# Weight splits of the last five experts moved to the second half of row 1, the clearing of the sorted rows moved to row 2, and twelve matmuls on cleared rows ahead of TensorE's first turn

## What is computed

```python
x = x + attn(layernorm(x))      # logits = Q K^T / sqrt(8); attn = sin(30 * logits) V; then Wo, bo
def expert(x, Wg, Wu, Wd): return silu(x @ Wg.T) * (x @ Wu.T) @ Wd.T     # 128 -> 256 -> 128
probs = sigmoid(x @ Wr.T + rb); scores, idx = top_k(probs, 2)
x = x + expert_shared(x) + sum over e of cw[..., e] * expert_e(x)         # x after a second layernorm
```

## Time and profile before

| | us |
|---|---|
| median of 3 runs | 456.49 |
| the profiled execution | 458.69 |
| span of the profiled execution, first to last instruction | 456.9 |
| PE busy in the span | 419.2 |
| ACT busy | 337.6 |
| DVE busy | 294.0 |
| POOL busy | 236.7 |

### The profile page before, as it was taken

How to read it: one execution, slowest core, us unless ns; L and a number is a source line. 1 busy time by engine, 2 the same in 40 slices (tenths; PEclk the granted TensorE clock), 3 DMA queues, 4 the chain that set the end, 5 groups by cost and what they waited for, 6 DMA issues and landing times.

```text
span 456.9 us, 12398 instructions
## 1 busy us (share of the span) xinstructions
PE 419.2 (92%) x4432; PEld 220.9 (48%) x4432; DVE 294.0 (64%) x999; ACT 337.6 (74%) x470; POOL 236.7 (52%) x308
## 2 busy tenths in 40 slices
PE   2899989999999999999999999999999988999972
PEld 1322222433433345554454455554544588998862
DVE  6778487456546254758676457786475567667894
ACT  1567968988989978788868887778788656765440
POOL 5261352120177333224867585426685778678851
PEclk9999989999999999999999999999999999999995
DMA  6027868917506642684246724992112256651221
GB/s 173 6 82 201 181 183 241 296 33 227 107 24 177 170 94 66 174 199 82 80 133 199 133 72 145 188 196 70 48 49 63 59 104 153 148 147 42 70 60 34
DMA packets 82187, 56.07 MB, mean 123 GB/s; under 512 B 28752, under 2 KB 76496, under 8 KB 82128
## 3 DMA queue, kind: packets, MB, share of 16 engines
q1 hardware_dynamic: 77824, 47.74, 41.6%
q0 software_dynamic: 3584, 7.35, 6.0%
q10 hardware_dynamic: 720, 0.20, 0.2%
HBM read 22.62 MB, written 27.13 MB: 109 GB/s over the span
## 4 chain that ended last, share of the span: by engine, by line
PE 63%; DVE 14%; issue 8%; ACT 7%; DMA 2%; POOL 2%; SPq 1%; DVEq 0%; ACTq 0%; POOLq 0%
PE o_ps L754 19%; PE score L741 10%; ACT attn L1018 4%; PE tile_ps L881 4%; PE tile_ps L883 4%; PE tile_ps L882 4%; PE tile_ps L906 3%; DVE hid L1351 2%; DVE x_all L1397 2%; PE r_ps L767 2%; DMA y_back<-in_wd 2%; PE r_ps L697 2%; PE r_ps L704 2%; PE tile_ps L908 2%; PE tile_ps L907 2%
## 5 line engine op out<-in xcount | busy, mean ns | idle before, releaser
L1018 ACT ACTIVATE attn<-score 128x1024 f32<-128x1024 f32 x237 | 231.7, 1031 | 22.5 <-PE score L741 22.1
L1576 POOL TENSOR_TENSOR hid_lo<-hid,hid_hi 128x256 f16<-128x256 f32 (+1 forms) x94 | 71.7, 763 | 128.0 <-DVE hid_hi L1359 116.4
L754 PE MATMUL o_ps<-attn,vals 128*32 128x512 f32 x1024 | 136.8, 606 | 0.5 <-ACT o_t L1025 0.5
L741 PE MATMUL score<-queries,keys 64*128 64x512 f16 x474 | 76.8, 384 | 4.6 <-ACT attn L1018 3.6
L1351 DVE SCALAR_TENSOR_TENSOR hid<-tile_ps,gate 128x256 f32<-128x256 f32 (+1 forms) x88 | 40.4, 459 | 49.3 <-ACT gate L1039 47.7
L1039 ACT ACTIVATE gate<-tile_ps 128x256 f32<-128x256 f32 (+1 forms) x88 | 36.3, 412 | 35.1 <-PE tile_ps L883 33.7
L881 PE MATMUL tile_ps<-xt,w_hi 128*128 128x128 f16 x244 | 43.7, 219 | 0.7 <-ACT y_sb L1051 0.7
L754 PEld LDWEIGHTS o_ps<-attn,vals 128*32 128x32 f32 x1024 | 20.2, 108 | 49.1 <-issue 48.0
L883 PE MATMUL tile_ps<-xt,w_lo 128*128 128x128 f16 x244 | 43.7, 219 | 0.0
L882 PE MATMUL tile_ps<-xt,w_hi 128*128 128x128 f16 x244 | 43.7, 219 | 0.0
L1044 ACT ACTIVATE hid_hi<-hid 128x512 f16<-128x512 f32 (+1 forms) x38 | 23.1, 607 | 27.8 <-DVE hid L1351 27.8
(11 more groups left out here) (226 smaller groups left out, 997.5 us busy)
## 6 DMA issues: line engine op xcount, KB each, us to landing
q_four<-q_parts SPq DMA_DIRECT2D x14, 256.0 KB
queries<-q_four SPq DMA_DIRECT2D x14, 256.0 KB
k_four<-k_minus SPq DMA_DIRECT2D x14, 256.0 KB
keys<-k_four SPq DMA_DIRECT2D x14, 256.0 KB
y_sorted<-y_sb SPq DMA_DIRECT2D x52, 64.0 KB
x_sorted<-zeros SPq DMA_DIRECT2D x2, 1472.0 KB, 8.5
queries<-q_three SPq DMA_DIRECT2D x14, 192.0 KB
keys<-k_three SPq DMA_DIRECT2D x14, 192.0 KB
```

Source lines behind the costliest of these rows:

```text
L741: mm = pe.matmul(sets[which][:, i, :], keys[b % 2][rows, 2 * j + h, kt * P:(kt + 1) * P], queries[b % 2][rows, 2 * j + h, :], start=True, ...
L754: mm = pe.matmul(o_ps[32 * i:32 * i + 32, :], vals[b % 2][:, kt, h:h + 32], attn[k % RING][:, i, :], start=(k == 0), stop=(k == UNITS - 1))
L1018: act.activation(attn[k % RING][:, 2 * (u % 2):2 * (u % 2) + 2, :], sets[SCORE_SET[b * SLOTS + u][0]][:, :, :], ACT.Sin, scale=SIN_SCALE). ...
L1576: pool.tensor_tensor(cells(hid_lo, d), cells(hid, d), cells(hid_hi, d), ALU.subtract).then_inc(lo_by_pool, 1)
```

## The change

The nine preparation slots, evenly spaced before (12, 16, ... 44), become a list: 12, 16, 20, 24 as before for experts 0 to 3, and 46, 49, 54, 56, 62 for experts 4 to 8. With them move the splits (two slots later) and the loads of experts 6, 7 and 8 (now at slots 49, 52 and 57, before at 31, 35 and 39). The two clears move from slots 48 and 50 to 66 and 68. PE gets a wait on a new semaphore, set when POOL has cleared `vals[0]`, and then 12 f32 matmuls of 128x128 on that cleared buffer into r_ps, whose result the first transposes overwrite.

```diff
-PREP_FIRST, PREP_EVERY = 12, 4
+PREP_AT = (12, 16, 20, 24, 46, 49, 54, 56, 62)
+PREP_FIRST = PREP_AT[0]
...
+WARM = 12
...
 def prep_at(a):
-    e, off = divmod(a - PREP_FIRST, PREP_EVERY)
-    return e if 0 <= e < EXP and off == 0 else None
+    return PREP_AT.index(a) if a in PREP_AT else None
...
+        vals_clear = sem("vals_clear")
...
-                if a in (SLOTS + 16, SLOTS + 18):
-                    clear((a - SLOTS - 16) // 2)
+                if a in (2 * SLOTS + 2, 2 * SLOTS + 4):
+                    clear((a - 2 * SLOTS - 2) // 2)
...
+            pe.wait_ge(vals_clear, 1)
+            for _ in range(WARM):
+                pe.matmul(r_ps[:, 0:P], vals[0][:, 0, 0:P], vals[0][:, 0, 0:P], start=True, stop=True)
             pe.wait_ge(ld_id, 16)
             xt1(0)
...
-            pool.memset(vals[0][:, :, :], 0.0)
+            pool.memset(vals[0][:, :, :], 0.0).then_inc(vals_clear, 1)
```

## The result

The changed kernel takes 455.09 us in the median of 20 runs (454.02 to 457.48), the kernel before 456.33 in 20 runs (455.33 to 458.16). The ratio is 0.9967, with a 95% interval of 0.9954 to 0.9980: faster by a third of a percent, about 1.5 us, where 6.1 us were forecast. The time lies above the range of 449.0 to 454.0. In a second comparison, with 12 executions of the changed kernel, the ratio was 0.9985 (0.9963 to 1.0007), which does not exclude no change. Ratios are taken from the executions that did not run in the slow state.

The account below looks back on a forecast made before the run. PE was taken to bound the kernel, busy 419.2 of 456.9 us. Start 2.4, seam 3.72, middle of row 1 0.38, late splits -0.4 summed to 6.1 us, taking the median from 456.49 to 450.4; range 449.0 to 454.0.

Parts of the forecast that it names:

- The seam: Between rows 0 and 1: PE's pause goes (2.13 us) and the clock does not fall (1.59), together 3.72 us.
- the late splits: Splits of experts 6 to 8, second half of row 1: PE may wait before its second `down`; 0.4 us lost.
- the median, 2.2 us below it, becomes 456.49 - 6.1: Final step: the whole 6.1 us, summed from the profiled execution, is taken off the median, giving 450.4 us.
- rival B: Row 1 to row 3's copy: late weights of experts 7 and 8 hold DVE again; 454.6 us, chance 0.14.
- Expert 8 at nothing: Before row 3's copy: expert 8's weights are rounded before DVE comes, so its split costs nothing.
- The burst: Start: twelve matmuls raise PE's clock early and it stays; first scores 2.4 us earlier, bounds 0 and 2.7.
- Rival A: Start: the clock is not there when the projections come; 451.4 us, or 452.8 with nothing won; chance 0.25.
- The middle of row 1: Without the split between pack_hi and pack_lo, `xt2` follows its scores; 0.38 us won, bounds 0 and 0.70.
- The clears: Issued behind expert 8's load and x's, they run from about 90 us in a stretch without q and k loads; worth 0.
- C: Row 1's key transfer or a later row waits for something fixed and the gain is given back; 456.5 us, chance 0.05.
- D: Slow loads of experts 7 and 8 hold DVE's list and PE behind it; slower, 458.9 at 10 us landing; chance 0.06.

Follow-up runs that it names:

- experiment 3: The kernel before, unchanged, run and profiled once more; ratio 0.9984 (0.9942 to 1.0025).
- again: The changed kernel, unchanged, run and profiled a second time; ratio to before 0.9985 (0.9963 to 1.0007).
- experiment 4: Changed kernel with experts 7 and 8 rounded and split in row 2 (slots 78, 81); ratios to before 0.9905, 0.9922, 0.9893 in three comparisons.
- experiments 2: The kernel before plus only the twelve matmuls at the start and their semaphore; ratio to before 0.9967 (0.9932 to 1.0002).
- Experiment 7: Changed kernel with experts 7 and 8 rounded and split in row 2, without the twelve matmuls; ratio to before 0.9955 (0.9936 to 0.9973).
- experiment 8: The changed kernel without the twelve matmuls, keeping its own preparation list and moved clears; ratio to before 0.9987 (0.9965 to 1.0009).
- experiments 1: The kernel before with only the list of preparation slots changed, clears and start as before; ratio to before 1.0140 (1.0074 to 1.0205).

## Why the prediction was wrong, point by point

- **The seam: right in mechanism, and in size for the execution it was read from.** Against the first profile of before the second stretch fell by 34.95 - 31.25 = 3.70 us; 3.72 were forecast. Against the second profile it is 2.06. The idle time is in all three profiles that had the pause (2.06, 1.93 and 1.73 us); the 1.59 of half clock in two of them (before and burst alone yes, before again no), and by the clocks in experiment 3 probably in fewer executions than that.
- **Two steps failed: the term of 0.4 us for the late splits, which cost 2.8 and is the largest error (next point), and "the median, 2.2 us below it, becomes 456.49 - 6.1".** In the second I took terms out of one execution and subtracted them whole from the median. The distance of 2.2 us was a warning: its size is that of the half clock (1.64) and the late rise (0.78) that I counted as gain. The typical run had lost less, so there was less to win. An estimate agrees: from the third marker to the end it is 352.5 us in the first profile of before, so the median of 456.33 has its third marker near 103.8, where the second profile has it (103.75, the first 106.18). For the seam the prediction gave 2.13 as the lower bound, for a clock that falls anyway; the case that came, by these signs, is a clock that in the typical execution of before does not fall at all. The sum should have said which terms hang on the clock and given them a chance.
- **The term mis-sized: the late splits, 0.4 us taken.** They cost 1.7 (changed), 3.2 (again) and 2.6 us (list and clears), the third stretch less 36.33: 2.5 in the mean. The middle's gain of 0.3 is already off these, so the late weights themselves cost 2.8; the medians of experiment 4 say 2.9. The mechanism of rival B and its landing were right: 89.4 on the clock of before was forecast, the first profile has 82.12 with 6.1 us won before it, 88.2. What was wrong is the middle value between 0 and 0.9, which had no row behind it, and the 1.30 us for a split: beside POOL's work it took 1.76 and, for expert 8 before row 3's copy, 2.37. The Trainium skill (SBUF — State Buffer, who interferes with whom) spoke for the longer one, and the trace agrees in direction: 1.76 is 1.30 plus 0.46, most of the one hidden_lo of 0.67 beside it, and 2.37 is 1.30 plus 1.07, most of the add of 1.27.
- **Expert 8 at nothing** was wrong for that reason: not its load (84.91, in time) but its split stood in the way, for 0.87 us.
- **The burst: 2.4 forecast.** 34.90 - 32.47 = 2.43 between the two profiles, and the first scores 2.49 earlier; but between the second profiles 0.54. Rival A's 0.25 fits what came: the rise was lost in 2 of 7 profiled executions with twelve matmuls. What was wrong is that 2.4 went into the sum whole, as if every execution kept it, and against one late rise: without a burst the clock rose anywhere from 13.0 to 16.2. The mean first kf is 34.27 in five profiles without and 32.79 in seven with it: 1.5 us, which is the 0.33% of experiments 2 and 7; experiment 8 gives less. The Trainium skill (TensorE: Matmul & The Clock Gate, part 1) says that the switch point differs from run to run; these rows agree, and I should have priced the term by it.
- **The middle of row 1: right.** 36.33 - 36.04 = 0.29 against 0.38.
- **The clears, forecast at 0: wrong in kind.** Moving them without the list was not run. They are a condition of the list, worth about 7 us with it (experiments 1 and 8).
- **Rivals C and D.** Nothing was absorbed later: from the third marker to the end it is 352.5 us in the first profile of before and 352.4 to 352.9 in the five of other kernels on chips where before takes 456 us. D did not happen in the changed kernel, but in its list alone.

Summed again by means: burst 1.5, seam 2.1, middle 0.3, late weights -2.8: 1.1 us, and on top what the clock's fall at the seam took from before. By two profiles in three that is 1.1, and the sum 2.2 would lie above both measurements, 1.5 (0.9 to 2.1) and 0.7 (-0.3 to 1.7). By the four executions in 32 of experiment 3 it is 0.2, and 1.3 lies in both. Experiment 7 says the same: seam and middle give 2.4 and with two thirds of 1.6 it is 3.5, outside its 1.2 to 2.9. How often the clock falls there was not counted directly.

The version with experts 7 and 8 in row 2 beats both kernels.

## What to carry to other kernels

A profile is one execution. Before a term is subtracted from a median, ask what in it repeats: the idle time of a wait did, the half clock behind it did not. Work that is moved out of one engine's way lands in another's list: go through what stands behind it there, its read-outs for PE first, and through the transfers that its load will queue behind. And give moved work that is needed late a stretch that is late: here the weights had almost 60 slots to spare (the last split at slot 64, the first use at 123), and the last two were put where each stood before something of PE's.

## What the runs showed of the hardware that was not expected

- Matmuls on cleared rows raise the clock as others do: full from 5.6 to 8.1 us in the eight profiles with a burst that began at 2.62.
- The length of one pause did not decide whether the clock fell. It fell around pauses of 2.06, 1.93 and 2.01 us and stayed full through pauses of 1.73 and 2.16 us (the second profile of the changed kernel, before 89.00). At the start it stayed through 0.89 and 1.27 us in the first profile of the changed kernel and fell behind 0.88 and 0.84 us in the second.
- The second DMA (128 KB) of expert 7's weights landed 6.8 to 7.9 us after its issue behind the key loads in the four profiles in which DVE had to wait for it without the clears in front, and that of expert 8 2.5 us after it in the changed kernel, without key loads in front.
- The same program took 456 us on one chip and 478 to 480 on two others. The first 100 us agree within the clock's play; most of the difference arises after about 370 us: from row 7's residual to the first read-out of r_ps in the tail it is 41.8 us in the first trace of before (370.3 to 412.1) and 54.7 in the second (375.2 to 429.8). Its cause was not followed.
